# Third record of the tokenizer groups as rounded halves, and reordered engine lists, in a ViT tower with a mixture of experts

## The reference

```python
freq_bands = 2 ** [0 .. 5]                               # x: (4, 3, 512, 192)
xb = 2 * pi * x[..., None] * freq_bands
feat = concatenate([sin(xb), cos(xb)]).reshape(4, 512, 6912)
h = concatenate([cls_tok, einsum('bnf,of->bno', feat, W)])   # (4, 513, 192)

# linear attention, on layernorm(h); added to h
q = (elu(x @ Wq) + 1) * scale;  k = elu(x @ Wk) + 1;  v = x @ Wv
c = clip(cumsum(log(sigmoid(x @ Wf + bf))), -20, 20)
M = exp(c) * cumsum(exp(-c) * k v^T);  z = exp(c) * cumsum(exp(-c) * k)
out = layernorm((q M) / (q z)) * gamma + beta, then @ Wo

# mixture of experts, on layernorm(h); added to h
top 2 of 8 experts by softmax(x @ router_w), gates normalised
routed = sum of gate_e * (silu(x @ w_gate_e) * (x @ w_up_e)) @ w_down_e
shared = (silu(x @ ws_gate) * (x @ ws_up)) @ ws_down             # 768 wide
h + alpha * shared + (1 - alpha) * routed;  alpha = sigmoid(x @ sg_w + sg_b)
```

## Time and profile before

| what | value |
|---|---|
| timed runs, median of 3 | 547.55 us |
| the profiled execution | 548.59 us |
| its span | 546.8 us |
| mean granted clock of TensorE | 0.997 of full |
| TensorE busy | 534.0 us, 98% |
| VectorE busy | 363.8 us, 67% |
| ScalarE busy | 303.2 us, 55% |
| GpSimd busy | 193.9 us, 35% |
| whole records (L1481) | 1392 matmuls, 233.2 us |
| halved records (L1477, L1479) | 168 + 168 matmuls, 52.0 + 42.0 us |

### The profile page before, as it was taken

One profiled execution on the slowest core, in us unless ns is written; L12 is line 12 of the kernel. 1 busy time (PEld: TensorE's weight loads), 2 busy tenths in 40 slices (PEclk: granted clock), 3 DMA queues, 4 the chain that ended last, 5 costly groups with the idle time before them and its releaser, 6 DMA issues.

```text
span 546.8 us, 9142 instructions
## 1 busy us (share of the span) xinstructions
PE 534.0 (98%) x3251; PEld 501.8 (92%) x3251; DVE 363.8 (67%) x1034; ACT 303.2 (55%) x416; POOL 193.9 (35%) x212
## 2 busy tenths in 40 slices
PE   8999999999999999999999999999998999999997
PEld 8999999899999899999989999879886899999865
DVE  8847659655777657986953984658788256666437
ACT  4495456978647884668694872364232145544410
POOL 6235436232243312855212550003502324444400
PEclk9999999999999999999999999899999999999999
DMA  8910093010100001210000010601103532431174
GB/s 321 333 49 19 21 345 116 20 28 2 40 1 20 20 1 29 77 42 1 1 1 11 30 50 1 231 10 40 40 17 119 163 124 70 149 100 52 52 227 135
DMA packets 23488, 42.49 MB, mean 78 GB/s; under 512 B 2502, under 2 KB 15044, under 8 KB 23348
## 3 DMA queue, kind: packets, MB, share of 16 engines
q1 hardware_dynamic: 19560, 33.31, 18.5%
q0 software_dynamic: 3472, 8.07, 4.2%
q10 hardware_dynamic: 412, 0.53, 0.5%
HBM read 31.74 MB, written 14.79 MB: 85 GB/s over the span
## 4 chain that ended last, share of the span: by engine, by line
PE 75%; DVE 15%; ACT 7%; issue 2%; DMA 0%; ACTq 0%; DVEq 0%
PE ps L1481 30%; PE ps L1477 5%; PE ps L1725 4%; DVE feat L908 4%; PE ps L1778 2%; PE ps L1780 2%; PE ps L1479 2%; PE ps L1687 2%; PE ps L1689 2%; PE ps L1688 2%; PE ps L1691 2%; PE ps L1690 2%; ACT feat L560 1%; PE ps L1756 1%; PE ps L1757 1%
## 5 line engine op out<-in xcount | busy, mean ns | idle before, releaser
L1481 PE MATMUL ps<-w_tok,feat 128*128 128x192 f32 x1392 | 233.2, 327 | 1.6 <-ACT H L590 1.3
L1481 PEld LDWEIGHTS ps<-w_tok,feat 128*128 128x128 f32 x1392 | 226.1, 190 | 3.4 <-issue 3.4
L449 POOL TENSOR_SCALAR feat<-fx 128x512 int32<-128x512 f32 x108 | 96.0, 903 | 148.1 <-PE ps L1479 101.7
L908 DVE SCALAR_TENSOR_TENSOR feat<-fx,feat 128x512 f32<-128x512 f32 x102 | 72.9, 767 | 2.6 <-POOL feat L449 2.3
L554 ACT ACTIVATE feat<-feat 128x1536 f32<-128x1536 f32 x27 | 40.1, 1484 | 46.0 <-DVE feat L908 46.0
L557 ACT ACTIVATE feat<-feat 128x1536 f32<-128x1536 f32 x34 | 50.5, 1484 | 22.8 <-DVE feat L915 22.1
L495 POOL DMA_INDIRECT ydram<-yr,xs x39 | 37.8, 970 | 53.6 <-DVE yr L1247 53.6
L560 ACT ACTIVATE feat<-feat,half_pi 128x1536 f32<-128x1536 f32 x35 | 54.6, 1560 | 0.0
L1477 PE MATMUL ps<-w_r,X 128*128 128x384 f32 x168 | 52.0, 375 | 0.0
L489 POOL DMA_INDIRECT slots<-pay_a,posi x17 | 17.3, 1018 | 78.4 <-DVE posi L1173 75.0
L692 ACT ACTIVATE s_ring<-ps 128x512 f32<-128x512 f32 x24 | 14.4, 599 | 54.9 <-PE ps L1691 44.8
(11 more groups left out here) (322 smaller groups left out, 993.0 us busy)
## 6 DMA issues: line engine op xcount, KB each, us to landing
slots<-in_blank SPq DMA_DIRECT2D x1, 5031.0 KB, 19.6
w_tok<-in_wT SPq DMA_DIRECT2D x7, 576.0 KB, 9.4
fx<-in_xT SPq DMA_DIRECT2D x15, 256.0 KB, 2.8
xs<-slots SPq DMA_DIRECT2D x5, 645.0 KB, 7.8
yin<-ydram SPq DMA_DIRECT2D x8, 384.0 KB, 6.8
raw_a<-in_wea SPq DMA_DIRECT2D x4, 384.0 KB, 5.1
raw_b<-in_web SPq DMA_DIRECT2D x4, 384.0 KB, 5.6
w_tok<-in_wT SPq DMA_DIRECT2D x4, 288.0 KB, 7.5
```

Of the source, the lines that this page charges most:

```text
L449: ins = pool.tensor_scalar(feat[:, k % SLOTS, i, :].bitcast(I32), x[:, x_block(k), :], f_col[:, fi:fi + 1], 1.0, ALU.mult, ALU.mult)
L908: ins = dve.scalar_tensor_tensor(feat[:, s, i, :], x[:, x_block(k), :], f_col[:, fi:fi + 1], feat[:, s, i, :].bitcast(I32), ALU.mult, ALU. ...
L1481: return pe.matmul(out_, feat[:, k % SLOTS, i, tokens], w_tok[:, w_at(k) + i, :], start=(k == 0 and i == 0), stop=(k == NG - 1 and i == 5) ...
```

## The change

- R3 becomes 3: all three cosine records of the 21 groups are halved. The new rounded features go to `f_hi3`, two buffers that share the memory of `w_down`; so the load of `w_down` moves behind group 7 of the last image. The feature split and its rest are now two instructions each, one over 512 columns and one over 1024; the weight split grows from 2 to 3 records.
- The expert map's small arrays move into `xn_c`. The space for the descriptors of GpSimd's DMAs goes from 8192 to 4096.
- ScalarE, image 0: weight splits stand further ahead; the copies of the first image's tokens (`take_h(0)`) come before the cosines of image 1's group 0, and TensorE waits for sines and cosines of that group separately.
- VectorE: `feature_low(b, 4)` stands after `weigh_qk` and no longer at the end of `remainders(b, 5)`; `add_states` comes before `places(b - 1, [1])`; `gates(B - 1)` after `negatives` and `clip_odds`.
- TensorE, shared blocks: `router(B - 1, 1)` at block 1 and not 0; `router(B, 0)` and `ranks(B)` before the down product of their block, `router(B, 1)` after the one of Q_LG.

```diff
 NG3 = NG - 2
-R3 = 2
+R3 = 3
...
 wb = sb("wb", [P, NCS, 2, P], F32R)
+with nc.sbuf_tensor("f_hi3", [P, 2, T], F32R) as f_hi3:
+    pass
...
 posi = sb("posi", [P, 2, NT + 1, 2], I32)
-em_z, em_r, em_w = sb("em_z", [1, NTILE, NE - 1]), sb("em_r", [1, NTILE]), sb("em_w", [1, NTILE])
-emap, emapi = sb("emap", [1, NTILE]), sb("emapi", [1, NTILE], I32)
+em_r, em_w, emapi = (xn_c[0:1, 0, i * NTILE:(i + 1) * NTILE] for i in range(3))
+emapi = emapi.bitcast(I32)
+em_z, emap = sb("em_z", [1, NTILE, NE - 1]), sb("emap", [1, NTILE])
 f_hi = X23[:, 0, :, :].rearrange("p (s i) t -> p s i t", s=2)
+def high(k, i):
+    return f_hi3[:, k % 2, :] if i == 6 - R3 else f_hi[:, k % 2, i - 7 + R3, :]
...
     sp.dma_start(slots, blank).then_inc(blank_in, 16)
-    sp.dma_start(w_down[:, :, :].rearrange("p c d -> p (c d)"), wds).then_inc(wds_in, 16)
+    sp.wait_ge(tok_group, NG * B - 1)
+    sp.dma_start(w_down[:, :, :].rearrange("p c d -> p (c d)"), wds).then_inc(wds_in, 16)
...
         pool.wait_ge(tok_group, k + 1)
-        pool.tensor_tensor(w_r[:, w0 + 4:w0 + 6, :].rearrange("p i o -> p (i o)"),
-                           w_tok[:, w0 + 4:w0 + 6, :].rearrange("p i o -> p (i o)"),
-                           w_r[:, w0 + 6:w0 + 8, :].rearrange("p i o -> p (i o)").bitcast(F32),
+        pool.tensor_tensor(w_r[:, w0 + 6 - R3:w0 + 6, :].rearrange("p i o -> p (i o)"),
+                           w_tok[:, w0 + 6 - R3:w0 + 6, :].rearrange("p i o -> p (i o)"),
+                           w_r[:, w0 + 6:w0 + 6 + R3, :].rearrange("p i o -> p (i o)").bitcast(F32),
...
         act.wait_ge(wt_in[k], x_parts(k))
-        act.activation(w_r[:, w0 + 6:w0 + 8, :].rearrange("p i o -> p (i o)"),
-                       w_tok[:, w0 + 4:w0 + 6, :].rearrange("p i o -> p (i o)"), ACT.Copy).then_inc(whi_ready, 1)
+        act.activation(w_r[:, w0 + 6:w0 + 6 + R3, :].rearrange("p i o -> p (i o)"),
+                       w_tok[:, w0 + 6 - R3:w0 + 6, :].rearrange("p i o -> p (i o)"), ACT.Copy).then_inc(whi_ready, 1)
...
         act.wait_ge(sin_ready, 2 * (NG * a + k) + 2)
+        act.activation(high(k, 6 - R3), feat[:, k % SLOTS, 6 - R3, :], ACT.Copy)
         act.activation(f_hi[:, k % 2, :, :].rearrange("p i t -> p (i t)"),
-                       feat[:, k % SLOTS, 6 - R3:6, :].rearrange("p i t -> p (i t)"),
+                       feat[:, k % SLOTS, 7 - R3:6, :].rearrange("p i t -> p (i t)"),
...
     weight_high(1)
+    weight_high(2)
     sines(0, 4)
-    weight_high(2)
+    weight_high(3)
     sines(0, 5)
-    weight_high(3)
+    weight_high(4)
+    weight_high(5)
     sines(0, 6)
-    weight_high(4)
+    weight_high(6)
     sines(0, 7)
+    weight_high(7)
     split_hi_piece(0)
-    weight_high(5)
     split_hi_piece(1)
-    weight_high(6)
-    sines(1, 0)
+    sines(1, 0, (0,))
     attn8(0)
-    weight_high(7)
     take_h(0)
+    sines(1, 0, (1,))
...
         dve.wait_ge(fhi_ready, halves_before(a, k) + 1)
-        dve.tensor_tensor(f_lo[:, k % SLOTS, 6 - R3:6, :].rearrange("p i t -> p (i t)"),
-                          feat[:, k % SLOTS, 6 - R3:6, :].rearrange("p i t -> p (i t)"),
+        dve.tensor_tensor(f_lo[:, k % SLOTS, 6 - R3, :], feat[:, k % SLOTS, 6 - R3, :],
+                          high(k, 6 - R3).bitcast(F32), ALU.subtract)
+        dve.tensor_tensor(f_lo[:, k % SLOTS, 7 - R3:6, :].rearrange("p i t -> p (i t)"),
+                          feat[:, k % SLOTS, 7 - R3:6, :].rearrange("p i t -> p (i t)"),
...
                               None, ALU.bitwise_and).then_inc(r_ready, 1)
-        if a >= 1 and 2 <= k <= NG3 + 1:
+        if a >= 1 and 2 <= k <= NG3 + 1 and k != 5:
...
         weigh_qk(b)
+        feature_low(b, 4)
         attn3(b)
+        add_states(b)
             places(b - 1, [1])
-        add_states(b)
...
         if q == Q_QKV:
-            gates(B - 1)
             clip_odds(B)
+            gates(B - 1)
...
         if halved(a, k, i):
-            f = f_hi[:, k % 2, i - 6 + R3, tokens]
+            f = high(k, i)[:, tokens]
...
-            pe.wait_ge(sin_ready, 2 * q + 2)
+            pe.wait_ge(sin_ready, 2 * q + 1 + (5 in recs))
...
         up_one(q, 0)
-        if q == 0:
+        if q == 1:
             router(B - 1, 1)
-        if q == Q_LG + 1:
-            router(B, 1)
...
             attn8(B)
-        if q >= 2:
-            down(q - 2)
             ranks(B)
+        if q >= 2:
+            down(q - 2)
+        if q == Q_LG:
+            router(B, 1)
...
     arrays = {n: np.ascontiguousarray(a) for n, a in arrays.items()}
-    nc = bacc.Bacc("TRN2", target_bir_lowering=False, num_devices=1, dynamic_dma_scratch_size=8192)
+    nc = bacc.Bacc("TRN2", target_bir_lowering=False, num_devices=1, dynamic_dma_scratch_size=4096)
```

## The result

The changed kernel takes 549.14 us (median of 20 runs, 547.55 to 549.77) against 547.37 (20 runs) for the kernel before: ratio 1.0022, 95% interval 1.0016 to 1.0028. It is slower, by more than this measurement's 0.2% only just. I had forecast 546.5 and gave slower 0.19; the median lies above my whole range.

The account below looks back on a forecast made before the run. The prediction took TensorE, busy 98% of the span, as the bound, with little slack in several chains. Its terms, +0.2 +1.4 -0.7 -0.5 -1.4 = -1.0, took the median from 547.55 to 546.5 us (range 545.4 to 547.7).

Parts of the forecast that it names:

- Halving itself: Third halved record: TensorE saves 0.15 us per group, 3.2 us over 21; ScalarE pays 0.53 and VectorE 0.6 per instruction.
- Image 0 to 1: Start of image 1: tokens copied first, but TensorE's gain waited away at layernorm and the k rows; +0.2 us.
- Images 2 and 3: States' wait goes, but a new 2.5 us wait on the second layernorm appears; +0.7 us each, together +1.4.
- The router half: Shared-expert stretch: moving the router's second half one block removes a half clock level at 346 us; -1.4 us.
- Rival (c): The clock still falls once, or had not fallen in the timed runs; 547.9 us, chance 0.17.
- The gates: Shared-expert stretch: gates behind negatives let VectorE's chain start sooner, removing TensorE's wait on the SiLU; -0.7 us.
- The last router: Last image's router: halves moved around the down products, logits read 0.45 us earlier; -0.5 us.
- Rival (e): GpSimd's stores wait for descriptor space, 0.5 us beyond the cover in 39 tiles; 567 us, chance 0.02.
- Image 0: First image: larger weight halves fit in ScalarE's and GpSimd's idle time; 0 us.
- Rival (d): Slower through the layernorm behind group 5's low halves, contention in full: image 1 +1.1, images 2 and 3 +1.4 each; 548.8 us, 0.11.

Follow-up runs that it names:

- e3: The changed kernel with the remainders of group 5 moved from behind the places to ahead of weigh_qk; 540.81 us.
- e6: The changed kernel with two halved records as before and the remainders of group 5 early; 542.71 us.
- e7: e3 with ScalarE's powers ahead of the cosines of group 4; 540.05 us.
- e8: The kernel before with only the copies of the first image's tokens moved ahead of the last weight split and the cosines of image 1's group 0; 545.91 us.
- e4: The changed kernel with the low halves of group 4 back behind the remainders of group 5; 544.03 us.
- e14: The changed kernel itself measured again, nothing altered; 548.05 us in 11 runs.
- e5: The changed kernel with 6 extra matmuls on TensorE in front of the second layernorm wait in images 2 and 3; 548.48 us.
- e13: e3 with the remainders of group 5 late in image 2 alone; four runs at 544.11 to 544.60 us, two at 545.84 and 546.19.
- e11: e7 with the router's second half back at block 0, next to the first; median 540.38 us of four runs.
- e9: e7 with the gates of image 2 ahead of negatives and clip_odds again in the shared blocks; 540.44 us.
- e12: e7 with the remainders of group 5 back behind the places in image 2 alone; 541.80 us.
- e1: The kernel before with the third halved record and the memory it needs, all lists in the old order; 550.55 us.
- e10: e7 with the last image's router halves and ranks back in their old places around the down products; 540.54 us.

## Why the prediction was wrong

**Halving itself** was right: 0.63 us of high half and 0.69 of low half against my 0.53 and 0.6, both within bounds, and TensorE gains 0.15 us at each halved group. What it saves shows once nothing waits: 1.9 of 3.2 us (e3 against e6), 2.7 with the powers moved as well (e7).

**Image 0 to 1** is the first step that failed: +0.2 forecast, -2.60 measured. I wrote that whatever TensorE saved would be waited away at layernorm and at the k rows. e8 refutes it: both chains wait, directly or by VectorE's list, for what ScalarE does at that place, and move up with it. Layernorm was 2.2 us sooner and not 0.2. Three terms make up the difference: 0.9 for VectorE's start (81.12, not 82.0); 0.6 for contention on its remainders that did not come (1.94 us; GpSimd's rounding began at 82.39 and not at 81.5); and 0.6 for layernorm itself, of which two steps took 0.17 us each where before they took 0.48 and 0.63. Of the -2.60 this start is -1.56; the other -1.04 are the seven halved groups, which I had counted in part as waited away.

**Images 2 and 3**: mechanism and place were right, the size was not. I had a wait of 2.5 us; it is 2.3 and 2.0, plus 0.5 at L1491, which I had not named. Without the fall of the clock the two images cost 1.86 + 1.40 = 3.3 us against my 1.4. Counted from the start of image 2, as the forecast is, TensorE wanted layernorm 1.4 us earlier than before (I had 1.5), but layernorm ended 1.9 later and not 1.4, and L1617's step began 1.6 later and not 1.0; behind it another 0.2 was lost, where I had 0.3 given back. The term that was mis-sized is the low halves of group 4. I put them at nothing much since the places "were waiting until 208.35 anyway", and had the places 0.85 later and the sines 0.25. The places start 0.65 later, but the sines 0.94: at 212.66 in after, where before they stood at

```profile
213.56 1.49 ACT L554 ACTIVATE feat<-feat 128x1536 f32<-128x1536 f32 x1 [4.73 <-DVE feat L908]
```

and image 2 starts 1.84 us earlier in after. Undoing the move (e4) brings them 1.1 and 1.4 us forward: the price was in the sines, because the places did not get shorter by the 0.9 us that I had taken off for GpSimd's rounding.

**The clock behind the new wait** I did not see at all. The Trainium skill ("TensorE: Matmul & The Clock Gate", the HAM clock gate) says that the clock falls after idleness of TensorE, and I cited it only against my router term. A forecast of two waits of 2.5 us should have carried that price: 1.2 to 1.3 us per fall, in 12 of 20 and 4 or 5 of 11 runs. It moved the median from +0.5 to +1.8 us. The profiles of after and e14, with a fall behind a long wait, agree with that, and so does e5, where the filled wait brings none in 11 runs; that every such wait brings the fall they do not show, and e13's profile has the wait without it.

**The router half**: the mechanism exists (e11, 1 of 4 runs), but as a term of the sum it was wrong. The fall was in the profiled execution and, by their times, in two of the 20 runs of before. Rival (c) said just that and was right on this point. I also misread the trace. I wrote that in no image two router halves stand so close; the last image's do, from 405.92 to 409.37 us, with the same one product between them, and before's clock stays full there:

```profile
408.00:410.00 2.00, 2.00 (x16) 1.81 (x15) 0.48 (x3) 0.00 (x0) 0.00 (x0) 1.00 0.40 95
```

So this trace alone said that the pair need not bring the fall. Idleness does not account for it: TensorE was busy. What brings it is open.

**The gates**: zero for 0.7. I took VectorE's list for the bound where the operand was TensorE's. **The last router**: right, 0.45 for 0.5. **Rival (e)**, the smaller descriptor space: the 39 stores take 0.97 us each in after too, and no time is lost among them.

**Image 0**: +0.76 in after's profile, +0.26 to +1.03 in those of e3 to e5, e7 and e9 to e14, with the same lists there. A part of it, 0.08 to 0.33 us, is a wait at the first image's attention (L1622) that before does not have; the rest varies between executions.

In all, the lower group of runs is the profile's sum without a fall: 0.3 to 0.8 in image 0, -2.60, +1.86, +1.40 and -0.5 for the rest come to +0.4 to +0.9, and it lies at +0.5. The fall behind one of the waits adds the rest of +1.8. My -1.0 was off by +2.8: -2.8 in image 1, +1.9 in images 2 and 3, +1.3 for the new falls, +1.4 for the old one, +0.7 for the gates, and 0.3 or so in image 0. Rival (d) had the sign and nearly the time (548.8), by a wait that it had in the right place, but that was luck: it had image 1 at +1.1, not -2.60, and no fall of the clock.

## What to carry to other kernels

Where TensorE is 98% busy and several chains have under half a microsecond of slack, less work for TensorE can be worth nothing until the chain that it runs into is loosened: here the third record cost 6 us before one VectorE call was moved into an idle stretch, and brought 2 to 3 us after. Look for the engine that sits idle in front of the chain (ScalarE's 6.12 us) and ask which work of the blocking engine could have run earlier. Price a new wait of TensorE above its length, as the clock may fall behind it, and check a clock term found in one profile against the spread of the timed runs, and against other places of the same trace with the same pattern, before it goes into the sum.

## What was not expected of the hardware

The half clock level comes in some executions and not in others, and what decides is open: the same kernel, with the same waits to within 0.03 us, has it behind one wait or behind the other, or by its times and clocks not at all. Waits of 1.2 us brought none in nine runs (e4, e12); one of 3.9 us had it in its profile (e1).

It also comes with TensorE busy. The profiles of before, e11 and e10 have it, each time behind two router halves of 10 matmuls with 10 columns each and one gate product between them; those of e1 and e8, with the same order, do not. By their times it is in six of all 74 runs of before.

A fall can be free: e10's filled waits that TensorE would have had anyway. So a mean clock of 0.996 is no proof of lost time: five runs of before at 0.996 took 547.11 to 547.50 us, like those at 1.000. That their clock was low where e10's is, since before has the same order there, would fit; none of the five was profiled.
